# Moving the first attention's projections of the next batch into the head slots of this one

## The reference

```
x = x + tanh(g_xattn[0]) * L0_xattn(layernorm(x), ctx)   # "CoPE" attention, 16 heads of 16
x = x + tanh(g_ffn[0])   * L0_ffn(layernorm(x))          # 8 experts + 1 shared, top 2
x = x + tanh(g_xattn[1]) * L1_xattn(layernorm(x), ctx)   # "cross" attention
x = x + tanh(g_ffn[1])   * L1_ffn(layernorm(x))          # "gated" attention over x itself

# in L0_xattn, per head; Q, K, V are projections of layernorm(x), ctx, ctx
logits = Q @ K.T / sqrt(16)
gates  = sigmoid(logits)
pos    = minimum(flip(cumsum(flip(gates))), 63)
bias   = Q @ pos_emb looked up at floor(pos) and ceil(pos), interpolated
out    = softmax(logits + bias) @ V
```

## Time and profile before

| quantity | value |
|---|---|
| median of 3 runs | 5772.76 us (5771.01 to 5777.49) |
| profiled execution | 5764.52 us, span 5762.8 us |
| VectorE busy | 4173.9 us, 72% of the span |
| TensorE busy | 3495.9 us, 61% |
| ScalarE busy | 2277.9 us, 40% |
| GpSimd busy | 1398.1 us, 24% |
| mean granted TensorE clock | 0.712 of full |
| first masks of slot 0, core batches 0, 1, 2, 15 | 155.4, 364.4, 712.5, 5231.7 us |
| last instruction of the first core pass ends; SP's first load after it | 329.6; 331.3 us |

### The profile page before, as it was taken

One profiled execution on the slowest core, in us unless ns is written; L12 is line 12 of the kernel. 1 busy time (PEld: TensorE's weight loads), 2 busy tenths in 40 slices (PEclk: granted clock), 3 DMA queues, 4 the chain that ended last, 5 costly groups with the idle time before them and its releaser, 6 DMA issues. The chain is left out here.

```text
span 5762.8 us, 64716 instructions
## 1 busy us (share of the span) xinstructions
PE 3495.9 (61%) x21126; PEld 2255.5 (39%) x21126; DVE 4173.9 (72%) x9130; ACT 2277.9 (40%) x5185; POOL 1398.1 (24%) x1125
## 2 busy tenths in 40 slices
PE   3256575666657566565666656566565665656576
PEld 3133352433425344352433425334352443424353
DVE  3878597685967858597685967858588585967853
ACT  2434344343434434344343443434344343443432
POOL 0423123131222313223122221312223131321310
PEclk7577686766768677686776768677685776867676
DMA  3000000000000000000000000000000000000000
GB/s 114 0 8 1 10 1 1 10 1 10 1 10 1 1 10 1 10 1 1 10 1 10 1 2 8 1 10 1 10 1 1 10 1 10 1 1 10 1 6 2
DMA packets 42741, 41.52 MB, mean 7 GB/s; under 512 B 6468, under 2 KB 42342, under 8 KB 42360
## 3 DMA queue, kind: packets, MB, share of 16 engines
q1 hardware_dynamic: 33144, 28.46, 1.6%
q10 hardware_dynamic: 9216, 8.39, 0.5%
HBM read 32.64 MB, written 4.19 MB: 6 GB/s over the span
## 5 line engine op out<-in xcount | busy, mean ns | idle before, releaser
L663 PE MATMUL banks<-xn,w 128*128 128x256 f16 x6912 | 965.7, 306 | 228.6 <-ACT h L734 228.6
L585 DVE COPY_PREDICATED banks<-masks,banks 128x448 f32<-128x448 int16 (+5 forms) x1536 | 1031.0, 671 | 73.0 <-PE banks L381 12.4
L514 POOL TENSOR_TENSOR steps<-slope,rises 128x512 f32<-128x512 f32 x256 | 295.5, 1154 | 2762.9 <-DVE masks L577 2402.5
L663 PEld LDWEIGHTS banks<-xn,w 128*128 128x128 f16 x6912 | 746.0, 110 | 430.5 <-ACT h L734 253.7
L470 ACT ACTIVATE core_prob<-z,negmax 128x256 f32<-128x256 f32 x512 | 255.9, 503 | 580.7 <-DVE negmax L609 580.6
L554 DVE TENSOR_TENSOR_SCAN c<-gate,cap 128x514 f32<-128x514 f32 x256 | 323.6, 1264 | 182.7 <-ACT gate L446 182.7
L521 POOL TENSOR_TENSOR neg_rest<-shift,c 128x512 f32<-128x512 bf16 x256 | 298.3, 1165 | 463.6 <-DVE masks L577 423.0
L1091 DVE TENSOR_REDUCE row_negmax<-banks 128x2 f32<-128x512 f32 x512 | 337.9, 688 | 72.3 <-PE banks L294 58.8
L294 PE MATMUL banks<-h,eg_eth 64*128 64x256 f16 x1024 | 279.2, 404 | 182.0 <-DVE row_negmax L1091 168.7
L676 PE MATMUL banks<-w,a 128*128 128x256 f32 x1152 | 308.2, 415 | 103.9 <-DVE o L838 66.4
L525 POOL TENSOR_TENSOR partial<-partial,core_scores 128x512 f32<-128x512 f32 x256 | 365.9, 1429 | 1.2
(11 more groups left out here) (254 smaller groups left out, 6875.8 us busy)
## 6 DMA issues: line engine op xcount, KB each, us to landing
stage<-in_L_ffn_w SPq DMA_DIRECT2D x16, 512.0 KB, 5.1
z<-in_ctx ACTq DMA_DIRECT2D x32, 128.0 KB, 2.7
core_pT<-in_x ACTq DMA_DIRECT2D x32, 128.0 KB, 3.1
u<-in_ctx SPq DMA_DIRECT2D x32, 128.0 KB
x<-in_x SPq DMA_DIRECT2D x32, 128.0 KB
out<-x SPq DMA_DIRECT2D x32, 128.0 KB, 1.8
stage<-in_L_ffn_w SPq DMA_DIRECT2D x8, 256.0 KB, 6.7
stage<-in_L_ffn_sw SPq DMA_DIRECT2D x2, 512.0 KB, 4.4
```

Of the source, the lines that this page charges most:

```text
L514: nc.gpsimd.tensor_tensor(k.steps[:], k.slope[:], k.rises[:, h % 2], ALU.mult).then_inc(sem["core_steps"], 1)
L585: move = nc.vector.copy_predicated(tab[:, :, 0:S - b], k.masks[:, n, :, 0:S - b], tab[:, :, b:S])
L663: last = nc.tensor.matmul(k.bank[bank][:, f * S:(f + 1) * S], w[:, e, a, c, par, f * P:(f + 1) * P], k.x_parts[:, b, c, :], start=(n == 0) ...
```

## The change

The projections of the next batch's first attention leave the start of its own pass. They become a second set of generators, `ahead_tensor`, `ahead_scalar`, `ahead_vector` and `ahead_pool`, with nine pieces that are called at the end of the slots 8, 9, 10, 11, 12, 14, 15, 15 and 18 of the pass before (`AHEAD`), on all engines alike. They have four buffers of their own (`ahead`) and only bank 2 (the stacks alternate with bank 0, when the core's scores are done with it), so each piece waits for the one before to have emptied it. The core's transposes therefore go to bank 3, which they share with the weighted values. `run_pass` gets a third batch, `following`, whose loads SP issues at the start of the pass; there is one pass more at the front, for the projections of batch 0 alone, and the loop has 14 repetitions. The side has all its pieces in 16 slots (`SLOTS = H`, with tail0 and tail1 in slot 0). Beside this, within a slot: ScalarE computes the next head's gates and scores ahead of Exp and of the side pieces, TensorE the scores of head `s + 2` ahead of the later side pieces; `core_scores` has three buffers, `z` is written over `steps`, which has two; and the ring `pT` of the side's exponentials uses the idle tiles `xn`, `xT`, `ctxT` and `o` in place of `more_pT`.

```diff
-EARLY = 2
-SLOTS = H + 3
-PIECES = [0] * SLOTS
-PIECE_TIMES = PIECE_TIMES[EARLY:]
+SLOTS = H
+PIECES = [0] * (H + 3)
+AHEAD = [0] * (H + 3)
+for at in (8, 9, 10, 11, 12, 14, 15, 15, 18):
+    AHEAD[at] += 1
...
-def core_tensor(nc, k, pe, side):
+def ahead_tensor(nc, k, pe, heads):
+
     sem = k.sem
     pe.wait_ge(sem["core_loads"], 16 * 2 * NT)
-    transpose_tokens(nc, k, k.bank[0], k.core_ctx).then_inc(sem["core_ctxT_psum"], 1)
+    transpose_tokens(nc, k, k.bank[2], k.core_ctx).then_inc(sem["core_ctxT_psum"], 1)
+    yield
+    yield
     pe.wait_ge(sem["core_ctxT_ready"], 1)
+    pe.wait_ge(sem["core_xn_ready"], NT)
+    transpose_tokens(nc, k, k.bank[2], k.core_norm.xn).then_inc(sem["core_xT_psum"], 1)
+    yield
+    pe.wait_ge(sem["core_xT_ready"], 1)
     feature_projection(nc, k.wk_cope, k.core_ctxT, k.bank[2]).then_inc(sem["core_k_psum"], 1)
...
+    yield
     pe.wait_ge(sem["core_k_second"], NC)
+    feature_projection(nc, k.wq_cope, k.core_norm.xT, k.bank[2]).then_inc(sem["core_q_psum"], 1)
+    yield
+    pe.wait_ge(sem["core_q_second"], NC)
+    if heads:
+        pe.wait_ge(sem["core_scores_copied"], (NT + 1) * heads)
     for m in range(P // HB):
         if m >= 2:
             pe.wait_ge(sem["core_k_stack"], m - 1)
         stack_pair(nc, k, 1, k.core_k_parts, m, k.bank[2 - 2 * (m % 2)]).then_inc(sem["core_k_stack_psum"], 1)
...
+    pe.wait_ge(sem["core_q_stack"], P // HB)
+    if heads:
+        pe.wait_ge(sem["core_pv_done"], heads // 4)
+    token_projection(nc, k.wv_cope, k.core_ctxT, k.bank[2]).then_inc(sem["core_v_psum"], 1)
+    yield
...
-            transpose_tokens(nc, k, k.bank[2], k.core_prob).then_inc(sem["core_pT_psum"], 1)
+            if h >= 4 and h % 4 == 0:
+                pe.wait_ge(sem["core_o_ready"], h // 4)
+            transpose_tokens(nc, k, k.bank[3], k.core_prob).then_inc(sem["core_pT_psum"], 1)
+        if s + 2 < H:
+            raw(s + 2)
         for _ in range(PIECES[s] - FIRST[s]):
             next(side, None)
-        if s + 2 < H:
-            raw(s + 2)
         if s + 1 < H:
             table(s + 1)
...
+        for _ in range(AHEAD[s]):
+            next(ahead, None)
...
+        if s + 1 < H:
+            gates(s + 1)
+            keep_scores(s + 1)
         h = s - 2
         if 0 <= h < H:
             act.wait_ge(sem["core_z_ready"], NT * (h + 1))
...
         for _ in range(FIRST[s]):
             next(side, None)
-        if s + 1 < H:
-            gates(s + 1)
-            keep_scores(s + 1)
...
+            if following is not None:
+                for t in range(NT):
+                    sp.dma_start(k.core_ctx[:, t, :], k.ctx_rows(following, t)).then_inc(sem["core_loads"], 16)
+                    sp.dma_start(k.core_norm.x[:, t, :], k.x_rows(following, t)).then_inc(sem["core_loads"], 16)
...
-        run_pass(nc, k, 0, None)
-        with nc.Fori(1, B) as i:
-            run_pass(nc, k, i, i - 1)
-        run_pass(nc, k, None, B - 1)
+        run_pass(nc, k, None, None, 0)
+        run_pass(nc, k, 0, None, 1)
+        with nc.Fori(1, B - 1) as i:
+            run_pass(nc, k, i, i - 1, i + 1)
+        run_pass(nc, k, B - 1, B - 2, None)
+        run_pass(nc, k, None, B - 1, None)
```

More of the change, by code:

```diff
@@ L388, in core_tensor @@
     for s in range(H + 3):
-        for _ in range(FIRST[s]):
-            next(side, None)
         if s >= 6 and s % 4 == 2:
@@ L496, in core_scalar, with ahead_pool, core_pool @@
             nc.scalar.activation(whole(k.slope), k.bank[1][:], ACT.Copy).then_inc(sem["core_slope"], 1)
-def core_pool(nc, k, pool, side):
+        for _ in range(AHEAD[s]):
+            next(ahead, None)
+def ahead_pool(nc, k, pool):
+    yield
+    norm_pool(nc, k, pool, k.core_norm, "core_")
+    yield
+def core_pool(nc, k, pool, side, ahead):
     sem = k.sem
-    norm_pool(nc, k, pool, k.core_norm, "core_")
-    next(side, None)
-    next(side, None)
     for s in range(H + 3):
@@ L1162, in attention_vector, with run_pass @@
     yield
-def run_pass(nc, k, core, rest):
+def run_pass(nc, k, core, rest, following):
     sem = k.sem
+    heads = 0 if core is None else H
     with nc.Block() as block:
@@ L1182, in _ @@
             side = side_pool(nc, k, pool) if rest is not None else iter(())
+            ahead = ahead_pool(nc, k, pool) if following is not None else iter(())
             if core is not None:
-                core_pool(nc, k, pool, side)
+                core_pool(nc, k, pool, side, ahead)
+            for _ in ahead:
+                pass
             for _ in side:
@@ L1190, in _ @@
             side = side_tensor(nc, k, pe) if rest is not None else iter(())
+            ahead = ahead_tensor(nc, k, pe, heads) if following is not None else iter(())
             if core is not None:
-                core_tensor(nc, k, pe, side)
+                core_tensor(nc, k, pe, side, ahead)
+            for _ in ahead:
+                pass
             for _ in side:
@@ L1197, in _ @@
         def _(act):
+            side = side_scalar(nc, k, act) if rest is not None else iter(())
+            ahead = ahead_scalar(nc, k, act) if following is not None else iter(())
             if core is not None:
-                for t in range(NT):
-                    act.dma_start(k.core_ctx[:, t, :], k.ctx_rows(core, t)).then_inc(sem["core_loads"], 16)
-                    act.dma_start(k.core_norm.x[:, t, :], k.x_rows(core, t)).then_inc(sem["core_loads"], 16)
-            side = side_scalar(nc, k, act) if rest is not None else iter(())
-            if core is not None:
-                core_scalar(nc, k, act, side)
+                core_scalar(nc, k, act, side, ahead)
+            for _ in ahead:
+                pass
             for _ in side:
@@ L1210, in _ @@
             side = side_vector(nc, k, dve) if rest is not None else iter(())
+            step = stepper(dve, sem["dve_core"])
+            ahead = ahead_vector(nc, k, dve, step) if following is not None else iter(())
             if core is not None:
-                step = stepper(dve, sem["dve_core"])
-                core_vector(nc, k, dve, step, side)
+                core_vector(nc, k, dve, step, side, ahead)
+            for _ in ahead:
+                pass
             for _ in side:
```

150 lines of the change are left out of this document (81 added, 69 removed).

## The result

The changed kernel takes 5748.2 us (median of 5 runs, 5740.3 to 5757.8), against 5772.7 (5769.3 to 5777.5) for the kernel before, run beside it: a ratio of 0.9963, 95% interval 0.995 to 0.9975. That is 24.5 us faster where 176 were forecast. The profiled execution has a span of 5755.7 us, against 5762.8. It is the slowest of the changed kernel's five (5757.8), while the profiled one of the kernel before (5764.5) was quicker than all its five timed ones, so the two profiles lie closer together than the medians.

A forecast was written before the change was run, and what follows sets the result against it. VectorE or its waits bound the slots, chains of waiting engines the rest. Slots 306.8 plus end 28.9 gave 335.7 us a repetition instead of 348.1; -174 over 14, -4 and +2 at the ends: 5597 us, range 5460 to 5761.

The forecast's parts named there:

- the stretch behind M: From the last move of slot 15 (M) to the next slot 0's masks: 28.9 us instead of 74.2.
- the branch: TensorE's jump back to the loop's start, within the stretch behind M: 3.6 us.
- the waits for gates: VectorE's waits in the slots for the next head's gates: the 7.7 us go.
- slot 0's output projection: First attention's output projection, its side pieces now in slot 0: +4.7 us of VectorE waits.
- the logits' wait: VectorE's wait for the logits of gated attention's output, now in the slots: +2.8 us.
- v's price: The v projection added behind the last head's weighted values, after M: 3.9 us.
- The hand-over of k and q: VectorE waiting in the slots for the second parts of k's and q's projections: 2.5 us each.
- the 2.3 for gated attention's first scores: In the slots, first scores come one piece after the key stacks: +2.3 us of VectorE waits.
- the price of the two weighting chains: VectorE waits added in the slots: +8.2 us for cross attention's chain, +10.3 for gated attention's.
- a doubt of the projections: TensorE's clock in k's and q's projections: lower level 0.9 us more each, 25 in all; upper 25 less.
- the end of gated attention becomes the core's path: Rival: gated attention's chain in slots 13 to 15, priced 28 us; at 40.6 no gain. Slower, chance 0.14.
- It exchanges waits and nothing more: Rival: the 45.3 us saved behind M return as waits within the slots; 5761 to 5784 us, chance 0.04.

The follow-up runs named there:

- that of the weighting alone: The changed kernel with only the side pieces of slots 8 to 15, the two attentions, told off: 5695.4 us, ratio 0.9874.

## Why the prediction was wrong

Right were: the stretch behind M (28.9 forecast, 30.3 measured) with its parts, among them the branch; VectorE's work up to M (245.3; 245.5); the waits for gates gone; slot 0's output projection (+4.7 forecast; 4.6 stands there); the logits' wait (2.8; 2.5); v's price (3.9; 3.6). The hand-over of k and q was put too high (2.5 each; 0.4 and 2.2), the 2.3 for gated attention's first scores didn't come (row maxima wait 3.0 us, 3.3 before), and 3.2 us in which VectorE waits for an expert's product with w2 (`L883`) and 2.2 for gated attention's queries (`L1101`) weren't seen. Together these come to half a microsecond (-2.3 - 2.6 + 3.2 + 2.2).

The step that failed is the price of the two weighting chains in the slots' waits, "+8.2" and "+10.3", 18.5 together. In the slots 9, 10, 14 and 15 VectorE waits 21.5 us for tables and 7.0 for heads (means of 13 passes): 28.5, which is 10.0 more, and the slots came out 10.3 above the forecast. With 14 repetitions these 10.3 and the 1.4 us behind M are 164 of the 174 us forecast for the loop. I had kept the lengths that the chains had had elsewhere (27.3; 25 and 3) and put VectorE's work under them nearly right: 19 and 17.7, measured 18.2 and 16.6. But packed into a slot and a half a chain didn't keep its length. It took 32.8 us both times.

Shown is that the telling off sets this price: with the same work told off by hand the tables' wait goes from 21.3 to 0.8 us and the repetition from 347.4 to 334.7. That this is near the 335.7 of the forecast is chance. The slots are 7.4 us shorter than forecast there and the end 6.4 longer, and 5.0 us are VectorE instructions that run shorter, for which the forecast had no term.

What stretched the chains is only partly settled. Without the pieces ahead they take 28.3 and 29.2 us, so 4.5 and 3.6 come with those, where 3 were forecast; VectorE's waits for tables and heads are 23.5 us without them and 28.5 with them. Part may be the clock: in one kernel, that of the weighting alone, the cross chain takes 35.8 us in a pass with the clock at 0.60 and 32.3 in one at 0.66, the gated one 31.3 at 0.66 and 34.4 at 0.56, in the same stretch of the program (stage table, two passes each):

```profile
1211.90:1247.70 35.80, 25.48 (x178) 12.64 (x179) 26.03 (x60) 21.36 (x46) 12.43 (x11) 0.60 0.00 1
1901.20:1933.50 32.30, 23.93 (x180) 11.39 (x180) 25.72 (x61) 21.31 (x46) 11.61 (x11) 0.66 0.00 1
1317.30:1348.60 31.30, 22.19 (x180) 10.51 (x181) 19.14 (x41) 19.72 (x42) 9.46 (x8) 0.66 0.00 1
1657.60:1692.00 34.40, 25.55 (x180) 10.92 (x181) 19.16 (x40) 19.74 (x42) 9.46 (x8) 0.56 0.00 1
```

A late chain could also be the cause of the lower clock; no run held the clock and moved the chain. I had named a lower clock a doubt of the projections and not of the chains.

The rivals: "the end of gated attention becomes the core's path" had the mechanism that took the gain, with a price of 4.8 us a pass instead of 12.6, and shared by cross attention, for which I had none. "It exchanges waits and nothing more" is what the loop did: 43.4 us off its end, 43.2 more in its slots. The time of 5748 us still lies within the case that I had called the forecast (5460 to 5761), at its upper end. That speaks for the width of the range and not for the sum: the gain was a seventh of the 176 us.

That the new order helps is right for this kernel (83 us if half of it is undone), though gates and tables together waited 27.3 us without it and 21.5 with it, 5.8 less and not 7.7. As a rule it is wrong: in the kernel before, the new order costs 52 us (5766.1 to 5818.1), and the wait goes on to the table.

## What to carry to other kernels

A wait that is taken off one step of a chain of engines can come back at its next step, as it did here from the gates to the tables and from the tables to the heads: ask what the waiting engine does next and what stands ahead of that on the others. Work interleaved by slots should be told off by what it keeps the other engines from, not by its own length: a chain across three engines costs little where several slots of the busy engine lie beside it, and much where one slot holds it. When a change makes an interleaving denser, price the interleaving anew before judging the change; here the change was worth 24 us with the packing that came with it and 184 with another (5766.1 to 5581.7), of which that other packing alone gives 41 in the kernel before. And look at how long the busy engine's own instructions take before and after: part of what a packing gives can be instructions that no longer run beside another engine's.

## What the runs showed of the hardware

TensorE's granted clock was 0.60 and 0.55 of 2.4 GHz in the two weighting chains, against 0.75 and 0.77 before. These are means over whole stretches. In the cross chain TensorE worked 20.9 of 32.8 us where it had worked 20.2 of 27.3; in the gated one 25.4 of 32.8, where it had worked 16.0 of 22.1. So more waiting between its matmuls goes with the lower clock in the first and not in the second. The same stretch of the program ran 3.1 to 3.5 us longer at means of 0.56 to 0.60 than at 0.66. Passes of one loop in one execution can differ in this, though each runs the same program. TensorE's branch back to the loop's start took a median of 3604 ns, that of the other engines about 50. Two VectorE products of two tensors in SBUF (128x512, float32) took 1.64 us each time that GpSimd was in a tensor operation beside them (45 times each), and 0.68 to 0.69 us whenever it was not (99 times each).
